# Grouped convolution as one product per channel group on two column strips, staged through DRAM

## The reference, cut to what matters

```python
x = x + L0_ffn(L0_cond(x, cond))      # per-batch 32x32 mix; gate, up, down with 1792 units
x = x + L1_ffn(L1_cond(x, cond))      # grouped convolution; base product + LoRA of 2 of 8 experts
x = x + L2_ffn(L2_cond(x, cond))
x = x + L3_ffn(L3_cond(x, cond))

def L1_cond(x, c, weight, c_weight, bias):          # weight (32, 8, 9)
    out = lax.conv_general_dilated(x, weight, window_strides=(1,), padding=[(4, 4)],
        dimension_numbers=('NCH', 'OIH', 'NCH'), feature_group_count=4)
    return out + jnp.einsum('nd,od->no', c, c_weight)[:, :, None] + bias[None, :, None]
```

## Time and profile before

| | |
|---|---|
| median of 3 runs | 607.39 us (606.96 to 607.83) |
| profiled execution | 607.15 us |
| its span, first to last instruction | 605.1 us |
| mean granted TensorE clock | 0.997 |
| TensorE matmul busy | 580.8 us, 96% |
| VectorE busy | 253.3 us, 42% |
| GpSimd busy | 177.0 us, 29% |
| ScalarE busy | 134.1 us, 22% |
| DMA queue of SP | 49616 packets, 30.48 MB, 17.4% of 16 engines |

### The profile page before, as it was taken

The page is one execution under the profiler, slowest core; times in us unless marked ns, Lnnn a source line. Parts: engine busy times, 40 slices in busy tenths (PEclk is TensorE's granted clock), DMA queues, the critical chain, the costliest instruction groups (busy, mean ns, idle before and its releaser), DMA issues.

```text
span 605.1 us, 7782 instructions
## 1 busy us (share of the span) xinstructions
PE 580.8 (96%) x3009; PEld 459.2 (76%) x3009; DVE 253.3 (42%) x513; ACT 134.1 (22%) x230; POOL 177.0 (29%) x134
## 2 busy tenths in 40 slices
PE   7999999999999999999999999999999999976996
PEld 5788888788888888888888894858585798854774
DVE  4533425422227222253222232323223388867775
ACT  5222222222223222232222221101010023331232
POOL 2699952000002000020000025020200034558886
PEclk9999999999999999999999999999999999998999
DMA  8498200320002000010000172120401333111313
GB/s 291 167 412 304 75 2 0 75 81 0 0 0 87 0 0 0 0 18 0 1 0 1 42 279 58 29 58 17 139 0 18 87 88 87 19 18 18 119 61 117
DMA packets 51733, 41.86 MB, mean 69 GB/s; under 512 B 33024, under 2 KB 41984, under 8 KB 50944
## 3 DMA queue, kind: packets, MB, share of 16 engines
q1 hardware_dynamic: 49616, 30.48, 17.4%
q0 software_dynamic: 2016, 11.01, 5.1%
q10 hardware_dynamic: 80, 0.08, 0.0%
HBM read 23.44 MB, written 4.23 MB: 46 GB/s over the span
## 4 chain that ended last, share of the span: by engine, by line
PE 85%; DVE 9%; DMA 2%; issue 2%; POOL 1%; ACT 1%; SPq 0%; DVEq 0%; POOLq 0%
PE ps L470 84%; DMA xs<-in_x 2%; DVE c_lo L879 2%; DVE cT L879 2%; DVE rcat L1094 1%; POOL x_all L424 1%; DVE rest L1049 1%; PE ps L708 1%; DVE lg L879 1%; DVE ex L879 0%; DVE t L879 0%; DVE m L1045 0%; PE ps L652 0%; PE ps L614 0%; DVE rest L879 0%
## 5 line engine op out<-in xcount | busy, mean ns | idle before, releaser
L470 PE MATMUL ps<-c_lo,wl 128*128 128x512 f32 x448 | 175.9, 395 | 1.7 <-DVE c_lo L879 1.3
L470 PE MATMUL ps<-c_hi,wl 128*128 128x512 f32 x448 | 176.2, 397 | 0.2
L879 DVE TENSOR_TENSOR hff<-silu,ps 128x512 f32<-128x512 f32 x56 | 38.5, 687 | 171.1 <-PE ps L470 170.7
L470 PEld LDWEIGHTS ps<-c_lo,wl 128*128 128x128 f32 x448 | 84.0, 188 | 23.8 <-DVE c_lo L879 3.0
L470 PEld LDWEIGHTS ps<-c_hi,wl 128*128 128x128 f32 x448 | 84.1, 188 | 21.1 <-ACT c_hi L769 0.8
L470 PE MATMUL ps<-wl,h_hi 128*128 128x512 f32 x224 | 88.9, 397 | 0.0
L470 PE MATMUL ps<-wl,h_lo 128*128 128x512 f32 x224 | 88.8, 396 | 0.0
L879 DVE TENSOR_TENSOR cT<-ps,bias_bc 128x512 f32<-128x512 f32 x64 | 42.3, 685 | 82.7 <-PE ps L470 82.3
L363 POOL TENSOR_TENSOR c_lo<-cT,c_hi 128x512 fp32r<-128x512 f32 x8 | 10.7, 1342 | 181.3 <-ACT c_hi L769 181.3
L879 DVE TENSOR_TENSOR h_lo<-hff,h_hi 128x512 fp32r<-128x512 f32 x56 | 46.1, 824 | 39.1 <-ACT h_hi L769 39.1
L803 ACT ACTIVATE silu<-ps 128x512 f32<-128x512 f32 x56 | 33.5, 599 | 124.1 <-PE ps L470 124.1
(11 more groups left out here) (151 smaller groups left out, 609.2 us busy)
## 6 DMA issues: line engine op xcount, KB each, us to landing
wl<-in_wl POOLq DMA_DIRECT2D x14, 768.0 KB, 10.2
xs<-in_x SPq DMA_DIRECT2D x4, 1024.0 KB, 9.8
x_all<-in_x SPq DMA_DIRECT2D x1, 4096.0 KB, 14.9
stg<-x_all SPq DMA_DIRECT2D x64, 64.0 KB, 2.0
xs<-x_all SPq DMA_DIRECT2D x4, 1024.0 KB, 4.8
out_x<-x_all SPq DMA_DIRECT2D x16, 256.0 KB, 2.0
bias_bc<-bias_dram SPq DMA_DIRECT2D x15, 256.0 KB, 4.2
wbase<-in_wbase SPq DMA_DIRECT2D x1, 1024.0 KB, 5.0
```

What stands on the lines that cost most here:

```text
L470: return pe.matmul(o, l, r, start=start, stop=stop)
L879: return dve.tensor_tensor(o, a, b, op)
```

## The change

The convolution is taken by channel group. Output column t is split in even and odd (h), and for one group q of 8 channels the partition of `stg` holds (dt, channel in the group, s): 4 neighbouring values of t, 8 channels, 4 values of s, which is all that two neighbouring output columns need. So one product makes, for 16 batches and half of the pairs of t, all of (which of the two, s, output channel), 64 values: `wconv[:, q]` (128x64) is the stationary operand and 512 columns of `stg` the moving one. Two products, one for each half of the pairs, write to partitions 0 to 63 and 64 to 127 of bank 4 + q, without accumulation.

The result now stands channels on partitions, so VectorE transposes each bank in blocks of 32x32 into `tr` (`turn`), and then adds the bias from there (`add`). Its row order differs from the old one, so the rows of `war` and `wbase` are loaded in four quarters each.

The data gets to `stg` through DRAM: GpSimd copies each tile with even and odd t parted (`part`), SP stores it to `y_dram` (`put_back`), and `regroup` reads from there, in runs of 64 elements, each element twice (for two values of dt). The weights of the convolution go through DRAM as well, with 24 small loads into a `wconv` that GpSimd has zeroed. The loads of layer 1's weights wait for an earlier slice than before, and their tiles and some others share other space. `base_bias` no longer waits for the staging.

```diff
--- before.py
+++ after.py
@@ -44,6 +44,9 @@
+DT, CG = 4, 8
+Q = ROWS // CG
+WIN = 64
@@ -104,2 +107,3 @@
-        stg = sb("stg", [P, GB, P + 2])
-        wconv = sb("wconv", [P, CB, P])
+        stg = sb("stg", [P, Q, GB, WIN + 2])
+        wconv = sb("wconv", [P, Q, 2, S, CG])
+        tr = sb("tr", [P, 2, TOK])
...
+        y_dram = nc.dram_tensor("y_dram", (2, NB, ROWS * S, WIN), F32).ap()
+        w_dram = nc.dram_tensor("w_dram", (ROWS, S, CB * P), F32).ap()
+        halves_x = prod[:].rearrange("p j k o -> p (j k o)").rearrange("p (r h s c) -> p r h s c", r=2, h=2, s=S)
...
             def regroup(g):
-                sp.wait_ge(s_x_new[0], (g + 1) * GT)
+                for r in range(2):
+                    sp.wait_ge(s_y[r], 16 * 2 * (g + 1))
                 if g:
-                    sp.wait_ge(s_cond_mm[1], g * GT)
-                for s in range(S):
-                    for b in range(TB):
-                        src = x_all[b * ROWS:(b + 1) * ROWS, g * GT:(g + 1) * GT, s * P:(s + 1) * P]
-                        dst = stg[s * ROWS:(s + 1) * ROWS, b:GB:TB, 1:P + 1]
-                        sp.dma_start(dst, src).then_inc(s_staged[1], 16)
+                    sp.wait_ge(s_cond_mm[1], g * Q)
+                for dt in range(DT):
+                    at = 2 - (dt + 1) // 2
+                    for q in range(Q):
+                        src = y_dram[(dt + 1) % 2, g * GB:(g + 1) * GB, q * P // Q:(q + 1) * P // Q, :]
+                        sp.dma_start(stg[dt * ROWS:(dt + 1) * ROWS, q, :, at:at + WIN],
+                                     src.rearrange("b p c -> p b c")).then_inc(s_staged[1], 16)
+            def put_back(g):
+                for j in range(g * GT, (g + 1) * GT):
+                    sp.wait_ge(s_parted, j + 1)
+                    dst = y_dram[:, j * TB:(j + 1) * TB].rearrange("h b (c s) n -> (b c) h (s n)", s=S)
+                    sp.dma_start(dst, halves_x[:, j % 2].rearrange("p h s c -> p h (s c)")).then_inc(s_y[j % 2], 16)
...
-            sp.dma_start(wconv[:], A["wconv"]).then_inc(s_wconv, 16)
+            sp.dma_start(w_dram, A["wconv"].rearrange("(s i) c n -> i s (c n)", s=S)).then_inc(s_w_dram, 16)
+            sp.wait_ge(s_w_dram, 16)
+            sp.wait_ge(s_wconv_zero, 1)
+            for q in range(Q):
+                for cb in range(CB):
+                    for to in range(2):
...
+                        sp.dma_start(wconv[(cb + to) * ROWS:(cb + to + 1) * ROWS, q, to], src).then_inc(s_wconv, 16)
             for g in range(1, G):
                 bias(0, g)
                 sp.wait_ge(s_cond_mm[0], g * S)
                 sp.dma_start(xs[:], xd[:, g * GT:(g + 1) * GT, :]).then_inc(s_staged[0], 16)
+                put_back(g - 1)
                 if g == 1:
-                    sp.wait_ge(s_pad, 1)
+                    sp.wait_ge(s_pad, 2)
                     regroup(0)
             bias(1, 0)
+            sp.wait_ge(s_up, (G - 1) * M + 6)
+            for n in range(4):
+                at, h, to = n * ROWS, n // 2, n % 2
+                rows = slice(h * WIN + to, (h + 1) * WIN, 2)
+                for dst, src in ((war, "war"), (wbase, "wbase")):
+                    sp.dma_start(dst[at:at + ROWS], A[src][rows]).then_inc(s_weights1, 16)
+            for dst, src in ((bbase, "bbase"), (wlb, "wlb")):
+                sp.dma_start(dst[:], A[src]).then_inc(s_weights1, 16)
             sp.wait_ge(s_up, G * M)
-            for dst, src in ((war, "war"), (wbase, "wbase"), (bbase, "bbase"), (wlb, "wlb")):
-                sp.dma_start(dst[:], A[src]).then_inc(s_weights1, 16)
...
+            put_back(G - 1)
             for g in range(1, G):
                 regroup(g)
                 bias(1, g)
@@ gpsimd
-            with pool.Fori(1, G) as g:
+            def part(g):
+                pool.wait_ge(s_x_new[0], GT * (g + 1))
+                for j in range(g * GT, (g + 1) * GT):
+                    if j >= 2:
+                        pool.wait_ge(s_y[j % 2], 16 * (j // 2))
+                    pool.tensor_copy(halves_x[:, j % 2],
+                                     x_all[:, j, :].rearrange("p (s c h) -> p h s c", s=S, h=2)).then_inc(s_parted, 1)
+            for g in range(1, G):
                 block_diagonal(0, g)
                 split_c(g)
+                part(g - 1)
             block_diagonal(2, 0)
+            part(G - 1)
             def base_bias(g):
-                pool.wait_ge(s_weights1, 64)
-                pool.wait_ge(s_staged[1], STG * (g + 1))
+                pool.wait_ge(s_weights1, LOADS1)
...
+            pool.wait_ge(s_parted, NT)
             base_bias(0)
@@ tensor
-            def conv(g, j):
-                if j == 0:
+            def conv(g, q):
+                if q == 0:
                     pe.wait_ge(s_staged[1], STG * (g + 1))
-                for b in range(TB):
-                    for c in range(CB):
-                        ins = mm(bank(4 + j)[:, cols(b)], stg[:, j * TB + b, c:c + P], wconv[:, c],
-                                 start=c == 0, stop=c == CB - 1)
+                for h in range(2):
+                    ins = mm(bank(4 + q)[h * WIN:(h + 1) * WIN].rearrange("p (b a) -> p b a", a=ROWS),
+                             wconv[:, q].rearrange("p t r o -> p (t r o)"),
+                             stg[:, q, :, 1 + h * ROWS:1 + (h + 1) * ROWS])
                 ins.then_inc(s_cond_mm[1], 1)
             def layer0(g, more):
                 for m in range(M):
                     gate_up(g, m)
-                    if m >= 1:
+                    if m >= 1 and (more or m < M - 1):
                         down(g, m - 1)
...
-                    pe.wait_ge(s_wconv, 16)
-                    for j in range(GT):
-                        if j == 2:
-                            pe.wait_ge(s_h, g * M + M)
-                        conv(0, j)
+                    pe.wait_ge(s_wconv, WLOADS)
+                    conv(0, 0)
+                    conv(0, 1)
+                    down(g, M - 2)
+                    pe.wait_ge(s_h, g * M + M)
+                    conv(0, 2)
+                    conv(0, 3)
                 down(g, M - 1)
...
             def layer1(g, more):
...
-                    for j in range(GT - 1):
-                        conv(g + 1, j)
-                    pe.wait_ge(s_cT[1], GT * (g + 1) + 1)
+                    for q in range(Q - 1):
+                        conv(g + 1, q)
+                    pe.wait_ge(s_turned1, Q * (g + 1) + 1)
                     turn_hm(g)
-                    conv(g + 1, GT - 1)
+                    conv(g + 1, Q - 1)
@@ vector
             def cond1(g):
+                def turn(q):
+                    dve.wait_ge(s_cond_mm[1], Q * g + q + 1)
+                    if q >= 2:
+                        dve.wait_ge(s_cT[1], Q * g + q - 1)
+                    dve.transpose(tr[:, q % 2], bank(4 + q)).then_inc(s_turned1, 1)
+                def add(q):
+                    dve.wait_ge(s_turned1, Q * g + q + 1)
+                    t = tr[:, q % 2].rearrange("p (b s o) -> p s b o", s=S, o=CG)
+                    v = bias_bc[:].rearrange("p (b o) -> p b o", o=ROWS)[:, :, q * CG:(q + 1) * CG]
+                    o = cT[:].rearrange("p s (b o) -> p s b o", o=ROWS)[:, :, :, q * CG:(q + 1) * CG]
+                    tt(o, t, v.unsqueeze(1).broadcast_to([P, S, GB, CG]), ALU.add).then_inc(s_cT[1], 1)
                 dve.wait_ge(s_bias_bc[1], 16 * (g + 1))
-                v = bias_bc[:].rearrange("p (b o) -> p b o", o=ROWS)
-                for j in range(GT):
-                    dve.wait_ge(s_cond_mm[1], GT * g + j + 1)
-                    o = cT[:, :, j * P:(j + 1) * P].rearrange("p s (b o) -> p b s o", o=ROWS)
-                    tt(o, bank(4 + j).rearrange("p (b s o) -> p b s o", b=TB, s=S),
-                       v[:, j * TB:(j + 1) * TB].unsqueeze(2).broadcast_to([P, TB, S, ROWS]), ALU.add).then_inc(s_cT[1], 1)
+                for two in ((0, 1), (2, 3)):
+                    for q in two:
+                        turn(q)
+                    for q in two:
+                        add(q)
```

More of the change, by code:

```diff
@@ L87, in build @@
         condT, net_w0, net_b = views(pack_a, NB, 3 * HID, 6)
-        pack_d = sb("pack_d", [P, 3 * HID + 3 * K])
+        with ExitStack() as early:
+            pack_d = early.enter_context(nc.sbuf_tensor("pack_d", [P, 3 * HID + 3 * K], F32))
+            h1 = early.enter_context(nc.sbuf_tensor("h1", [P, 3, NB], F32))
+            h2 = early.enter_context(nc.sbuf_tensor("h2", [P, 3, NB], F32))
+            att_m = early.enter_context(nc.sbuf_tensor("att_m", [NB, 3, NT * K], F32))
         net_w1, net_w2 = views(pack_d, 3 * HID, 3 * K)
+        stg = sb("stg", [P, Q, GB, WIN + 2])
         pack_b = sb("pack_b", [NB, 3 * K + P + NT * K + ROWS])
@@ L94, in build @@
         wk = wk.rearrange("p (i k o) -> p i k o", i=3, k=K)
-        h1 = sb("h1", [P, 3, NB])
-        h2 = sb("h2", [P, 3, NB])
         att = sb("att", [NB, 3, K])
-        att_m = sb("att_m", [NB, 3, NT * K])
```

(48 more changed lines are left out.)

## The result

The changed kernel takes 581.62 us (median, 581.47 to 581.92) against 607.38 us (606.96 to 607.83): ratio 0.958 (95% interval 0.957 to 0.959), 25.8 us faster. Spans: 579.9 us after, 605.1 before, 25.2 us apart.

What follows compares the result with a forecast made beforehand. From 329.88 us through layer 1's turns the prediction took TensorE alone as the bound. Gains of 6.1 (end of layer 0) and 19.5 (turns) less stalls of 3.3 and 4.2 made 18.1 us: 589.3 us, range 583 to 603.

Steps and rivals of the forecast that it cites:

- TensorE comes free for `down(12)` at 344.65: End of layer 0: time read from the kernel before, from which the forecast counted the new convolution's first blocks.
- The end of layer 0: VectorE's last addition, not TensorE, starts `lora_a_router(0)`, at 353.0 instead of 359.11: 6.1 us gained.
- Turns without a stall: Layer 1's loop: strips side by side, less two mode round trips, save TensorE 6.49 us a turn, three times, 19.5.
- First stall: Group 1 of layer 1: `regroup(1)` lands at 373.8, TensorE wants it at 370.4 plus 0.1; 3.3 us lost.
- Second stall: Group 1 of layer 1: VectorE's additions wait for GpSimd's `base_bias`, TensorE stalls 4.2 us; bounds 0 and 9.0.
- Strips in series: Rival, convolution: the two strips run one after another, 3.44 us more per group, 600 us; chance 0.12.
- Slow small reads: Rival, `regroup`: 256 B packets cost more than the issue hides, gain gone at 46 ns; over 607.4 us, chance 0.10.
- Everything hidden: Rival, group 1: copies are quicker and GpSimd's work is over before the additions, 582 to 585 us; chance 0.05.
- Between: Rival: more collisions (9.0 instead of 4.2), packets at 34 to 46 ns, slow transposes, 594 to 607 us; chance 0.13.

Runs made afterwards that it cites:

- after_moved_32: The changed kernel with 32 unused bytes per partition ahead of `wl0`, no longer a multiple of 256 bytes from `c_hi`: 588.17 us, ratio 0.968.
- before_moved_32: The kernel before with an unused tile of 32 bytes per partition ahead of `wl0`: 598.43 us, ratio 0.985.
- half_runs: The changed kernel with `regroup` taking only half of each run, packets of 128 instead of 256 bytes and as many of them: 580.46 us.
- regroup_first: The changed kernel with `put_back(3)` moved behind `regroup(1)` and `bias(1, 1)` on SP: 576.49 us, ratio 0.949.
- bias_early: regroup_first with `base_bias` 0 to 2 ahead of the last copies and the fourth after the additions of group 1: 572.0 us, ratio 0.942.
- before_moved_160: The kernel before with 160 unused bytes per partition ahead of `wl0`: 605.23 us.
- one_strip: regroup_first with both halves of the convolution written to partitions 0 to 63, the second half's result lost: 588.46 us.

## Why the prediction was right or wrong, step by step

**What failed: "TensorE comes free for `down(12)` at 344.65".** The prediction took this time from the kernel before and let the sum start there: 6.1 + 19.5 - 3.3 - 4.2 has no term for what comes ahead of the convolution. The runs show 334.19 in its place, 10.5 us earlier. First, the diff resizes and moves tiles ahead of `wl0`, and with the distance to `c_hi` and `h_hi` a multiple of 256 bytes each of the 1344 fp32r records of layer 0 follows 0.0065 us sooner. By that product it is 8.7 us; the convolution starts 8.4 us earlier in the changed kernel than in after_moved_32, and 8.2 us earlier in before_moved_32 than before, whose time is 9.0 us less. Second, 2.1 us come from the changes of group, where GpSimd's new order takes `blk` out of VectorE's way. No term and no rival had either. Why such a distance is fast was not found; the runs show only that it decides. At the old step the changed kernel takes 588.2 us, inside the stated range and 1.1 below the forecast. That it comes so near is partly luck: there too the 2.1 us that had no term stand against stalls that were priced too low.

**The end of layer 0**: forecast 6.1 us, measured 6.4, and VectorE's last addition starts `lora_a_router(0)`, as forecast. The blocks are 2.01 us as records, 1.95 to the next product, for 2.08 forecast; transposes 0.712 us for 0.69; two additions 1.25.

**Turns without a stall**: forecast 25.54 us (32.03 less 6.49), measured 25.55. Strips side by side, the mode's round trip and the 0.43 us of a record were all right.

**First stall**: forecast 3.3 us, measured 7.38. `regroup(1)` started where it should (8.24 us behind `lora_a_router(0)`, forecast 8.5), but from there to the landing took 16.8 us instead of 12.3. The mis-sized term is the packet. These are windows of the changed kernel with a `regroup` in them, then with the wait and `conv(1)`:

```profile
113.00:123.00 10.00, 10.00 (x46) 8.29 (x45) 2.76 (x4) 2.46 (x4) 0.00 (x0) 1.00 1.28 159
352.00:362.00 10.00, 7.95 (x19) 3.23 (x17) 4.89 (x6) 0.00 (x0) 9.31 (x5) 1.00 1.36 162
362.80:367.30 4.50, 0.00 (x0) 0.00 (x0) 0.00 (x0) 0.00 (x0) 4.50 (x2) 0.50 1.21 135
367.30:372.60 5.30, 5.26 (x12) 1.25 (x12) 2.25 (x3) 0.00 (x0) 5.29 (x2) 0.50 0.01 1
```

Both stretches with a `regroup` run at about 160 GB/s, which looks like the limit of these packets: 2 MB take 13.1 us, and 8192 packets on 16 engines are 25.6 ns each, not 20. The forecast drew a line between 128 B from DRAM (13 ns) and 512 B from SBUF (34 ns), two kinds of source. Twice the 128 B row would have given 26, or, the same thing, 46 GB/s at a share of 0.28 is 164 GB/s at a full one. That the two agree is not proof: by the forecast's own formula, share x 16 x window / packets, the 256 B packet comes to 1.36 x 160 / 6328 = 34 ns, so the packets of an engine overlap and the share no longer gives the pace. half_runs agrees that the bytes count: half of them in as many packets were no longer the limit. The Trainium skill ("DMA: Bandwidth & Descriptors", Why small descriptors are slow) counts a fixed overhead of 3 cycles to 8 of data for 256 bytes; by it the 13 ns packet would grow by 11/7, to an estimated 20 ns. The trace doesn't agree: it grew to 25.6.

**What the stall does next** had no term: the clock. Within the wait, TensorE having been idle since 359.95, the granted clock falls to 0.50 (1.2 GHz), and `conv(1)` runs at it, 5.39 us instead of 2.91. A wait of 7.38 us cost 9.9.

**Second stall**: forecast 4.2 us, close to nothing in the changed kernel, since the late `conv(1)` let `base_bias` pass (it ended at 372.60, 30.3 us behind `lora_a_router(0)`; forecast 30.1). The mechanism is real: with `conv(1)` on time it cost 3.7 us of waiting and 1.5 of a slow router in regroup_first, and bias_early took it away for 4.5 us. The Trainium skill ("SBUF — State Buffer", Who interferes with whom) calls the port that VectorE and GpSimd share an exclusive lock; the 8.84 us for two additions beside 13.92 us of GpSimd agree.

Both stalls together: forecast 7.5 us, measured 35.68 - 25.54 = 10.1. With 0.3 more at the end of layer 0 and 1.0 lost behind the last turn (in layer 3 the granted clock is 0.77 in 519 to 534, against 0.89 in 545 to 560 before; no experiment was made, and the kernel before takes 128.5 us there in before_moved_160 and 130.5 in before_moved_32), the sum is 18.1 + 10.5 + 0.3 - 2.6 - 1.0 = 25.3, the span's 25.2.

**The rivals.** Strips in series: refuted by one_strip. Slow small reads: half true, 25.6 ns a packet, far from the 46 at which the gain is gone; `regroup(2)` and `regroup(3)` stayed hidden. Everything hidden (582 to 585): the measured time lies beside it, for another reason; what it means, both stalls gone, is bias_early, whose 572.0 us with the 10.5 of layer 0 added back are 582.5. Between (594 to 607) wanted slow transposes, which took 0.712 us, and packets at 34 ns and more.

## What to carry to other kernels

A diff that resizes buffers can change the pace of code that it doesn't touch: compare the step of unchanged products first, and if it differs, move a tile before explaining anything else. A new order on an engine that is off the path can also take away a short wait of the one that is on it. When two stalls stand in one turn, price the removal of both; removing one can give nothing (half_runs) or half (regroup_first). Price a small DMA packet from rows of the same source and by the rate, and add to a long wait of TensorE the work behind it at half clock.

## What the runs showed of the hardware

- fp32r products of 128x128x512 whose stationary and moving operand lie a multiple of 256 bytes apart in their partitions follow each other in 0.2268 us; at distances of 32, 96, 128 and 224 modulo 256 in 0.2333 to 0.2337, at 64 in 0.2327. An fp32 record of 512 columns (`wbase`) has a mean of 592 ns in all of these runs.
- Reads of 256 B packets from DRAM into SBUF ran at 159 and 162 GB/s in the two windows above, with the mean share of the 16 engines shown as 1.28 and 1.36; at a share above 1 packets overlap, so the rate, not the share, says what is left.
- Two column strips of 64 with 512 fp32 columns take 2.01 us for 8 records, one strip 3.80.
- VectorE's two splits of a group took 3.23 us with a GpSimd instruction of 1.49 us (`blk`) beside them and 2.38 without it, and TensorE waited 0.44 us for it at each of the three changes of group in the kernel before.
- After waits of 7.38 us (the changed kernel) and 6.43 us (half_runs) TensorE went on at a granted clock of 0.50; after 3.68 us (regroup_first) the router took 5.37 us instead of 3.87, with a mean clock of 0.73.
